# Splitting the routed rows of a mixture-of-experts stage into two parts, so that the first part returns inside the expert loop

## The reference, cut to what matters

```python
def _L0_ffn_ref(x, centroids, routing_bias, Wfc_r, Wproj_r, Wfc_sh, Wproj_sh):
    raw = jnp.einsum('bsd,ed->bse', x, centroids)                   # 8 experts
    routing_scores = jax.nn.sigmoid(raw)
    _, top_idx = jax.lax.top_k(jax.nn.sigmoid(raw + routing_bias), 2)
    gathered = jnp.take_along_axis(routing_scores, top_idx, axis=-1)
    top_w = jax.nn.softmax(gathered, axis=-1)
    combine = jnp.sum(jax.nn.one_hot(top_idx, E) * top_w[..., None], axis=-2)
    h_sh = gelu(jnp.einsum('bsd,nfd->bsnf', x, Wfc_sh))              # 2 shared experts
    shared_out = jnp.einsum('bsnf,ndf->bsd', h_sh, Wproj_sh)
    h_r = gelu(jnp.einsum('bsd,efd->bsef', x, Wfc_r))
    expert_out = jnp.einsum('bsef,edf->bsed', h_r, Wproj_r)
    routed_out = jnp.einsum('bsed,bse->bsd', expert_out, combine)
    return x + shared_out + routed_out
x = x + _L0_ffn_ref(_layernorm(x), ...)
```

## Time and profile before

| | us |
|---|---|
| median of 3 runs | 1369.81 (1367.13 to 1371.88) |
| profiled execution, its own time | 1372.54 |
| its span, first to last instruction | 1370.7 |
| busy PE / DVE / ACT / POOL | 1168.1 / 852.0 / 640.9 / 584.2 |
| mean granted clock of PE | 0.917 |

### The profile page before, as it was taken

The page is one execution under the profiler, slowest core; times in us unless marked ns, Lnnn a source line. Parts: engine busy times, 40 slices in busy tenths (PEclk is TensorE's granted clock), DMA queues, the critical chain, the costliest instruction groups (busy, mean ns, idle before and its releaser), DMA issues. The chain is left out here.

```text
span 1370.7 us, 31685 instructions
## 1 busy us (share of the span) xinstructions
PE 1168.1 (85%) x11577; PEld 975.8 (71%) x11577; DVE 852.0 (62%) x1811; ACT 640.9 (47%) x1125; POOL 584.2 (43%) x604
## 2 busy tenths in 40 slices
PE   6576999799999999279999999984899888999950
PEld 4355666678999966268888888874566678999950
DVE  4396788775222224268888888872687666666751
ACT  3201677442566542055655656640677521456620
POOL 0356232401773077424334344335233212775475
PEclk9799999889999999689999999996999967999985
DMA  4001221410232111200000000000000050233232
GB/s 128 14 1 24 69 50 45 158 65 9 81 90 62 37 50 53 94 1 1 1 0 0 0 0 0 0 1 14 16 18 17 4 207 17 77 84 72 70 107 64
DMA packets 60720, 61.67 MB, mean 45 GB/s; under 512 B 12417, under 2 KB 49793, under 8 KB 60113
## 3 DMA queue, kind: packets, MB, share of 16 engines
q1 hardware_dynamic: 50000, 41.74, 10.2%
q0 software_dynamic: 8864, 18.17, 5.2%
q10 hardware_dynamic: 1760, 0.49, 0.2%
HBM read 42.22 MB, written 16.06 MB: 43 GB/s over the span
## 5 line engine op out<-in xcount | busy, mean ns | idle before, releaser
L1861 PE MATMUL f_bank<-f_xT,f_w_tile 128*128 128x128 f32 x1192 | 159.8, 277 | 0.9 <-DVE f_xT L1705 0.9
L1873 PE MATMUL f_bank<-f_w_down,f_hidden 128*128 x1192 | 159.4, 277 | 1.2 <-ACT f_hidden L1783 1.1
L1524 POOL DMA_INDIRECT f_xn<-f_xn_rows,f_source x149 | 142.9, 959 | 39.9 <-issue 39.2
L1861 PEld LDWEIGHTS f_bank<-f_xT,f_w_tile 128*128 128x128 f32 x1192 | 146.7, 194 | 1.5 <-DVE f_xT L1705 1.3
L1873 PEld LDWEIGHTS f_bank<-f_w_down,f_hidden 128*128 128x128 f32 x1192 | 146.2, 193 | 1.8 <-issue 1.7
L1535 POOL DMA_INDIRECT f_hot_row<-f_slots_y,f_slots x128 | 122.1, 954 | 38.1 <-issue 38.1
L957 POOL TENSOR_TENSOR ret_rstd<-ret_var,ret_minus_half 128x8 f32<-128x8 f32 x32 | 52.7, 1647 | 169.8 <-DVE ret_var L1008 169.8
L752 DVE TENSOR_REDUCE a_top<-a_scores 128x16 f32<-128x1024 f32 x64 | 78.4, 1224 | 55.2 <-PE a_scores L823 55.0
L1771 ACT ACTIVATE f_w_tile<-f_w_up 128x512 f32 x149 | 91.9, 619 | 30.7 <-DVE f_owner L1675 29.6
L716 POOL TENSOR_TENSOR X<-X,a_mixed 128x128 f32<-128x128 f32 x64 | 29.1, 454 | 158.6 <-DVE a_mixed L744 158.1
L1471 DVE SCALAR_TENSOR_TENSOR X<-f_hot_row,f_weights,X 128x128 f32<-128x128 f32 x128 | 37.2, 348 | 92.0 <-DMA f_hot_row<-f_slots_y,f_slots 91.5
(11 more groups left out here) (289 smaller groups left out, 2888.2 us busy)
## 6 DMA issues: line engine op xcount, KB each, us to landing
f_slots_y<-f_y_out SPq DMA_DIRECT2D x73, 128.0 KB, 2.0
a_v_rows<-in_ctx SPq DMA_DIRECT2D x16, 256.0 KB, 3.9
f_xn_rows<-f_xn SPq DMA_DIRECT2D x16, 256.0 KB, 11.2
f_w_up<-in_f_up SPq DMA_DIRECT2D x1, 2560.0 KB, 9.3
f_w_down<-in_f_down SPq DMA_DIRECT2D x1, 2560.0 KB, 16.6
f_xn<-f_xn_rows,f_source POOLq DMA_INDIRECT x149, 2.5
kv_ctxT<-in_ctxT SPq DMA_DIRECT2D x8, 256.0 KB, 2.8
X<-in_x SPq DMA_DIRECT2D x4, 512.0 KB, 9.3
```

Of the source, the lines that this page charges most:

```text
L1524: pool.indirect_dma_start(out=x_in[:, s % RING, :], out_offset=None, in_=xn_rows[:, :], in_offset=bass.IndirectOffsetOnAxis(ap=source[:, s ...
L1861: last = pe.matmul(bank_h[m % 2][:, j * P:(j + 1) * P], w_tile[m % W_RING][:, j * P:(j + 1) * P], xT[m % 2][:], start=True, stop=True)
L1873: last = pe.matmul(bank_y[m % 2][:, 0:D].unsqueeze(1), hidden[m % 2][:, j, :], w_down[:, bass.ds(expert + E0, 1), j, :], start=(j == 0), s ...
```

## The change

The first feed-forward stage gets the two parts that the last one has. The one-hot products of part 1 go to a PSUM bank of their own (bank 6; part 0 keeps bank 4, since bank 4 is in use by the loop when part 1 is collected). PE collects only groups 0 to 4 before the loop. The additions of groups 0 to 2 move into the loop, and their `bn_stats` stay behind it.

```diff
-        bank_s = bank[4] if E0 else bank[6]
+        bank_s = [bank[4], bank[6]] if E0 else [bank[6], bank[6]]
...
-                    dve.tensor_copy(source[:, start[part]:start[part + 1]], bank_s[:, 0:counts[part]])\
+                    dve.tensor_copy(source[:, start[part]:start[part + 1]], bank_s[part][:, 0:counts[part]])\
...
-                for m in range(len(ADDED_AT) if parts > 1 else 0, GROUPS):
+                for m in range(GROUPS):
                     if shared and m >= FIRST_UNITS // 2:
                         add_shared(m)
-                    for quarter in range(4):
-                        add_rows(dve, m, quarter)
+                    if parts == 1 or m >= len(ADDED_AT):
+                        for quarter in range(4):
+                            add_rows(dve, m, quarter)
                     if not spec["last"]:
                         dve.wait_ge(added[1], GTILES * (m + 1))
...
-                            last = pe.matmul(bank_s[:, 0:counts[part]], hot_row[q % 2][:, n, t, :],
+                            last = pe.matmul(bank_s[part][:, 0:counts[part]], hot_row[q % 2][:, n, t, :],
...
                         for q in COLLECT.get(place, ()):
-                            collect(q)
+                            if q < first_group[1]:
+                                collect(q)
...
-    ffn_phase(g, "f0", dict(kind="sigmoid", plus_xn=True, part_tiles=(32,), last=False, shared=2, gelu=ACT.Gelu, gate_w="f0_gate_w",
+    ffn_phase(g, "f0", dict(kind="sigmoid", plus_xn=True, part_tiles=(20, 12), last=False, shared=2, gelu=ACT.Gelu, gate_w="f0_gate_w",
```

## The result

The changed kernel runs in 1365.94 us (median of 16 runs, 1360.89 to 1368.61), the kernel before in 1372.97 (16 runs on the same chips, 1367.13 to 1377.17). The ratio is 0.9948, 95% interval 0.9935 to 0.9962: 7.0 us or 0.5% faster. The time forecast, 1368.1, is near the measured one, and that lies inside the range. The size of the change was not forecast well: -1.7 us, against -7.0. "Within 0.3%" had the largest chance, 0.59, and it came out as "faster by more", with 0.22.

The account below looks back on a forecast made before the run. PE was taken to bound the first stage's loop, and eight reads of 10.3 us its tail. Terms -5.2 - 3.3 + 13.3 + 8.2 - 14.7 = -1.7 us turned the median 1369.8 into 1368.1 us; range 1364 to 1374.5.

Parts of the forecast that it names:

- Within 0.3%: Whole kernel: a change under 0.3% (4.1 us), which a measurement can't tell from none; chance 0.59.
- faster by more: Whole kernel: faster by more than 0.3% (4.1 us); chance 0.22.
- collects out of the prologue: Before the first stage's loop: three of eight collects leave, 1.74 us of PE each, -5.2 us.
- first five passes: Start of the first stage's loop: an earlier index removes PE's three waits for rows, -3.3 us.
- seven passes and three collects: First stage's loop: seven more passes of 1.896 us, +13.3 us, and three collects inside it, +8.2 us.
- tail, to the last statistics: Behind the first stage's loop: PE becomes the bound instead of reads, 74.2 us in place of 88.9, -14.7 us.
- the chain that the prediction had named: Loop start: DVE's third shared addition and first copy might replace the removed waits, making that gain 0 instead of 3.3 us.
- "faster" rival: First stage's loop: collects do not wait, three cost 5.3 us in place of 8.2; 1365.2 us, chance 0.16.
- rival of blocked additions: First stage's loop: additions held by the port rule or late reads, +10 - 1.7, giving 1378 us; chance 0.06.
- rivals of one fall or more: PE's clock falls behind collects in the loop: once, 1371.2 us, chance 0.25; more often, 1374.3 to 1377.4, chance 0.11.

Follow-up runs that it names:

- p1_no_adds: Changed kernel with no additions inside the first stage's expert loop, the two parts kept; 1366.15 us, ratio to the kernel before 0.9951.
- e1_reads8: Changed kernel with eight more indirect reads by POOL at the end of the first feed-forward stage; 1370.34 us.
- e3_pool_late: Changed kernel with one small POOL addition at the first feed-forward stage's end, waiting for DVE's last addition; 1376.96 us.
- e4_before_dve16: Kernel before with 16 more DVE statistics at the end of the first feed-forward stage; 1368.39 us.
- e2_reads4: Changed kernel with four more indirect reads by POOL at the end of the first feed-forward stage; 1366.58 us.
- e7_pool_waits: Changed kernel with POOL waiting at the end of both feed-forward stages for its last rows to land; 1367.69 us, ratio to the kernel before 0.9974.
- e6_read_elsewhere: Changed kernel with one indirect read by POOL, waited for, at the start of the attention stage before the first feed-forward stage; 1375.35 us.

## Why the prediction was right and wrong

| step | forecast | measured in the profile |
|---|---|---|
| collects out of the prologue | -5.2 | (334.67 - 257.08) - (339.14 - 255.86) = -5.69 |
| first five passes | -3.3 | 342.69 - 334.67 = 8.02, was 350.32 - 339.14 = 11.18: -3.16 |
| seven passes and three collects | +13.3 + 8.2 | 491.77 - 342.69 = 149.08, was 127.95: +21.13 |
| tail, to the last statistics | -14.7 | 566.12 - 491.77 = 74.35, was 88.93: -14.58 |
| boundary behind the stage | not in the sum | 0.66, was 4.89: -4.23 |
| sum | -1.7 | -6.53 |

**What held.** The four terms inside the stage came within 0.5 us each, by rows of the kernel before. The index copy of part 0 stood at 324.3 (forecast 323), and the first passes lost their waits for rows; in place of them PE waited once, 0.83 us, for DVE's copy, which stood behind DVE's third shared addition, the chain that the prediction had named. The collects waited 0.40 to 0.44 us in place of 0.50, 0.3 us less for the three together: that is all that came of the "faster" rival, which wanted no waits and 2.9 us less. The tail became bound by PE, 74.35 us where 74.2 were worked out. DVE's pairs of additions in the loop took 0.60 to 0.66 us beside POOL's reads, and the passes kept their 1.896 us, so the rival of blocked additions did not come, and p1_no_adds shows the additions to be free. The clock kept 1.00 in loop and tail, against the rivals of one fall or more. That the first stage would keep it was a judgement and not shown beforehand: in the last stage, with the same collects, the changed kernel's products fell to the lower clock behind the second collect, where the kernel before had its fall behind the third.

**What failed.** "It was 567.20 - 478.27 = 88.9. Gain 14.7.": the step *The tail* ended at DVE's last statistics, and the sum went on as if the next stage followed at a fixed distance. The distance was 4.89 us before and 0.66 after. Before, the stage ended with POOL: 562.31 + 9.74 = 572.05. After, it ended with DVE. The rivals did not hold it either: each asked what could go wrong inside the stage. With the boundary the step is 88.93 + 4.89 - 74.35 - 0.66 = 18.8 us and not 14.6, and with it the sum would have been near -6, "faster by more". e1_reads8 and e3_pool_late put the cost back, e4_before_dve16 fills the gap for nothing, and e2_reads4 stays under the point from which it shows.

**What was luck.** That the time came so near. 1368.1 was added up from the median of three runs, 1369.81; sixteen runs of the same kernel give 1372.97. From that the sum of -1.7 would have said 1371.3, 5.3 us too slow. The low start hid most of the boundary's 4.2 us, and the range, 1364 to 1374.5, was laid around it too.

**What stays open.** The prologue gained 0.5 us more than the three collects were priced at, and this was not taken apart. The 1.49 us behind the stage are within the spread of equal code and were not tested. Why 135 reads and more always leave 9.7 us in a feed-forward stage is open, as said.

## What to carry to other kernels

End a sum at the first instruction of the next stage and not at the last of this one: read the gap there on every engine, and ask which engine sets it. An engine that was done early can be the last, when something stands behind its last instruction; then a change that only lets it finish earlier pays more than the busy rows say, and a trifle added to its end costs all of it (0.19 us of POOL cost 8.4). Of a change in two parts, try each part alone: here the earlier reads paid, and the additions in the loop that went with them did not matter. And measure the kernel before as often as the changed one: a median of three runs was 3.2 us off here, more than the change that was forecast.

## What the runs showed of the hardware

- Behind POOL's last instruction of a stage with 135 to 150 indirect reads lay 9.66 to 9.74 us before POOL's next, at every boundary where POOL was last, and 9.7 us between the last read and the end of the kernel in every run but e7_pool_waits (11.5 with POOL's wait for the landing in it). At the ends of the attention stages, without such reads, it was 0.95 to 1.20, and DVE's own gap may have set that.
- In an attention stage the gap was 0.95, 1.99, 5.91 and 2.97 us behind 1, 16, 64 and 141 reads, though all had landed some 120 us before; the last came with a standing of 4.40 us behind the 113th read.
- Behind 16 indirect reads that all fetch the same row of memory POOL stood for 8.6 to 9.6 us from the end of the last one until they had landed (8.66 above), and 3.00 behind a single one (e6_read_elsewhere). A group's last read of different tokens' rows was used by DVE 1.6 us behind its end (1354.22 and 1355.77 in the changed kernel's last stage). That the shared row is the cause was not tested.
